# Attention with relative positions and a mixture of experts: reciprocals in another step, first keys in float32, two copies on GpSimd

## The chip, the cores and the metric

The kernel runs on one core of one Trainium2 chip. The metric is the device time of one execution in microseconds (us), less being better. Five engines work side by side: TensorE (PE) multiplies, VectorE (DVE), ScalarE (ACT) and GpSimd (POOL) compute element by element, and SyncE (SP) issues most transfers.

## The reference, cut to what matters

x is 16 x 512 x 128 in float32; there are 16 heads of 8 columns.

```python
Q, K, V = heads(xn @ Wq.T + bq), heads(xn @ Wk.T + bk), heads(xn @ Wv.T + bv)  # xn = layernorm(x)
scores = einsum('bhld,bhrd->bhlr', Q, K) / sqrt(8) + einsum('bhld,lrd->bhlr', Q, rel_k)
attn = softmax(scores)
out = einsum('bhlr,bhrd->bhld', attn, V) + einsum('bhlr,lrd->bhld', attn, rel_v)
x = x + out @ Wo.T + bo
x = x + shared_experts(layernorm(x)) + top2_of_8_experts(layernorm(x))  # exact gelu, hidden 256
```

rel_k[l, r] and rel_v[l, r] are rows of a table chosen by r - l; distances beyond the table take its last row.

## The kernel before

**Stages.** The 16 batches are worked off in 8 pairs. Each pair takes 16 steps of 32 queries, each step two rounds (s, j) with j = 0 or 1. A round makes four score tiles of 128 rows (8 heads and 4 queries in each of two batches) by 512 keys. After the last pair the experts run batch by batch. Products need float32 accuracy, so most operands are split into a high and a low f16 half, and three matmuls are added up (`projected`).

**A round.** `scores` on TensorE (lines 1545, 1527, 1534) fills banks 0 to 3. VectorE takes each tile's negated maximum (line 1030, `maxima`), ScalarE the exponential with its row sum (line 793). TensorE meanwhile multiplies the values and relative values of an older step (lines 1612 and 1622), transposes the probabilities of the round before (line 1592), and VectorE and ScalarE copy these out of PSUM (lines 1035 and 783). TensorE's last transpose of a round carries the waits for the next scores (`next_scores_wait`). GpSimd spreads the queries into the stationary tiles stat_hi, stat_lo and stat_rel of a later step (lines 557, 567, 573).

**Pieces.** Some rounds have one further piece of work in bank 1, which starts once the second exponential of the round has read that bank (`round_read`). In (0, 1) and (1, 0) it is this pair's value projection (lines 1507 to 1509), in (8, 0) and (8, 1) the transposes of the next pair's normalised rows (line 1469, then ScalarE's copy in line 716 and VectorE's subtraction in line 970), later its keys and queries. The last pair has no next one; its pieces, from (7, 0), belong to the first batch's experts, and the one in (7, 1) needs the reciprocals.

**Row sums.** Each pair's row sums lie in one of two buffers. `reciprocals` on VectorE makes their reciprocals in three dependent instructions (lines 1225, 1228, 1230): the reciprocal, the high f16 half, the low half. It runs for the pair before at the end of round (0, 1). ScalarE waits for it once, at the start of a pair, for the buffer that was done a pair ago.

**The start.** For pair 0 all is done in one piece. TensorE transposes the rows and projects queries, then keys in f16 (lines 1474 to 1476) and transposes natural queries (line 1492). ScalarE copies the keys out of PSUM (line 756) into `first_k`, and from there makes k_hi with two biases (lines 761, 762); VectorE makes q_hi's rest q_lo (line 997), splits the queries (lines 1010, 1012), and makes k_lo from `first_k` (lines 1002, 1003); GpSimd makes the low part of q_split (line 547). The sync queue brings q_hi's halves into q_twice in four transfers for the first 128 queries of each batch (line 384), then q_lo's (line 387), then keys. The first scores wait for stat_rel, which needs q_rel (lines 776, 1017) from VectorE and ScalarE. VectorE does head_scaled (line 1354) on the way.

The order is written out by hand; every engine has its own queue and works it off in order, held only by semaphores.

Of the kernel before, what the change touches and what calls it, by code (L numbers as in the profile page):

```python
# [107 lines left out]
def attention_ffn(nc, x, w_qkv, cols, rows, wo_t, bo, rk_win, rv_win, rw, rb, w1, w2, b2,  # L108
                  sw1, sw2, sb2, b1_cols, consts, rel_scratch, out):
    with ExitStack() as ctx:  # L110
# [43 lines left out]
        mv = sb("mv", [P, 8, 2])  # L154
        var_eps = sb("var_eps", [P, 8])
        rstd = sb("rstd", [P, 8])
        xn_t = sb("xn_t", [P, TOK])

        xn_split = xn_t[:].bitcast(F16).rearrange("p (a c) -> p a c", a=2)
# [31 lines left out]
        probs_t = [sb(f"probs_t{i}", [P, QUADS, RT, P]) for i in range(2)]  # L191


        first_k = attn_t[:, TOK:2 * TOK].rearrange("p (b c) -> p b c", b=2)

        w1_s = attn_t[:, 3 * TOK:3 * TOK + EXPERTS * HID].rearrange("p (e h) -> p e h", e=EXPERTS)
        w2_s = attn_t[:, 3 * TOK + EXPERTS * HID:3 * TOK + 2 * EXPERTS * HID].rearrange("p (e k d) -> p e k d", e=EXPERTS, k=2)
# [46 lines left out]
        loaded, w1_loaded, w2_loaded, ffn_loaded = sem("loaded"), sem("w1_loaded"), sem("w2_loaded"), sem("ffn_loaded")  # L244
        w_high, w_low, ffn_setup = sem("w_high"), sem("w_low"), sem("ffn_setup")
        qkv_high, qkv_low, xn_low = sem("qkv_high"), sem("qkv_low"), sem("xn_low")
        setup_dve = sem("setup_dve")
        setup_pool = sem("setup_pool")

# [67 lines left out]
        def _(sp):  # L317
# [56 lines left out]
                    cols = slice((4 * twos + a) * P, (4 * twos + a + 1) * P)  # L374
                    sp.dma_start(rel_scratch[bass.ds(row, 32), cols], rel_t[32 * a:32 * a + 32, twos % 2, :]).then_inc(rel_stored[twos % 2], 16)

            def first_queries(cols, landed):
                def part(rows):
                    return rows.rearrange("p (b c) -> p b c", b=2)[:, :, cols]

                sp.wait_ge(hi_ready, START + 2)
                for half in range(2):
                    for copy in range(2):
                        sp.dma_start(part(q_twice[64 * copy:64 * copy + 64, half, :]), part(q_hi[64 * half:64 * half + 64, :])).then_inc(landed, 16)
                sp.wait_ge(q_low_ready, START + 2)
                for half in range(2):
                    sp.dma_start(part(q_lo_pair[64 - 64 * half:128 - 64 * half, 1, :]), part(q_lo[64 * half:64 * half + 64, :])).then_inc(landed, 16)
# [93 lines left out]
                load_rel(b)  # L481


            first_queries(slice(0, P), first_q_landed)
            first_keys(sp, 1, slice(0, L), first_k_landed)
            first_queries(slice(P, L), q_copies_landed)
            for b in range(2):
                first_keys(sp, b, slice(L, KEYS), k_copies_landed)
            pair_windows(0, 0, True, True)
# [20 lines left out]
        def _(pool):  # L510
# [100 lines left out]
            def pair_steps(pair, first, ahead):  # L611

                if first:
                    pool.wait_ge(first_q_landed, COPIES * 16)
                else:
                    pool.wait_ge(q_copies_landed, START + (pair + 1) * COPIES * 16)
                for s in range(STEPS):
                    if first and s == GROUP_STEPS:
                        pool.wait_ge(q_copies_landed, START + COPIES * 16)
                    if s >= 2 or not first:  # L620

                        pool.wait_ge(score_done, START + (pair * STEPS + s - 1) * QUADS)
                    if s == STEPS - 1:

                        spread_relative(s)
                        spread_high(s)
                        spread_low(s)
                    else:
                        spread_high(s)
                        spread_low(s)  # L630
                        if s == 0:
                            pool.wait_ge(q_rel_ready, START + pair * 4 + 4)
                        spread_relative(s)
                    if s == 2:
                        for b in range(2):
                            far_values(pair, b)
                    chunk = chunk_in(pair, s, 3)
                    if chunk is not None:
                        low_weights(chunk)
                    if not ahead and s in (3, 4):  # L640
                        spread_heads(s - 3)
                    if ahead and s == 8:
                        deviations(pair + 1)
                        normalised(pair + 1)
                    if ahead and s == 14:
                        split_low(pair + 1, 0)
                    if ahead and s == 15:
                        for b in range(2):
                            low_queries(pair + 1, b)
                        split_low(pair + 1, 1)  # L650
                    if not ahead and s == 12:
                        deviations_after(0)
                    if not ahead and s == 15:
                        gate_exponentials(0)

            deviations(0)
            for i, split in enumerate((wq_split, wk_split, wv_split)):
                pool.wait_ge(qkv_high, i + 1)
                nc.gpsimd.tensor_tensor(split[:, 1, :], w_qkv_s[:, i, :], split[:, 0, :], ALU.subtract).then_inc(qkv_low, 1)
            pool.wait_ge(setup_dve, SETUP_FIRST)  # L660
            for b in range(2):
                split_low(0, b)
            pair_steps(0, True, True)
# [47 lines left out]
        def _(act):  # L711
# [38 lines left out]
                act.wait_ge(q_ready, START + b + 1)  # L750
                nc.scalar.activation(q_hi[:, b * L:(b + 1) * L], q_f[:, b * L:(b + 1) * L], ACT.Copy).then_inc(hi_ready, 1)

            def first_plain_keys(b, bank):

                act.wait_ge(proj_done, START + 2 + b + 1)
                nc.scalar.activation(first_k[:, b, :], ps[:, bank, :], ACT.Copy, scale=1.0 / W_SCALE).then_inc(k_ready, 1)

            def first_high_keys(b):

                act.wait_ge(k_ready, START + b + 1)  # L760
                nc.scalar.activation(k_hi[0][:, b, FAR_COLS:KEYS], first_k[:, b, :], ACT.Identity, bias=bks_col[:, 0:1])
                nc.scalar.activation(k_hi[0][:, b, 0:FAR_COLS], first_k[:, b, FAR * P:L], ACT.Identity, bias=bk_far_col[:, 0:1]).then_inc(hi_ready, 1)

            def high_weights(n):

# [125 lines left out]

            act.wait_ge(loaded, 16 * LOADS)

            for i, (split, scale) in enumerate(((wq_split, 1.0), (wk_split, SCALE), (wv_split, 1.0))):
                nc.scalar.activation(split[:, 0, :], w_qkv_s[:, i, :], ACT.Copy, scale=W_SCALE * scale)
                nc.scalar.activation(w_qkv_s[:, i, :], w_qkv_s[:, i, :], ACT.Copy, scale=W_SCALE * scale).then_inc(qkv_high, 1)
            for half in range(2):
                rows_t(0, half, half)
            nc.scalar.activation(rk_split[:], rk3, ACT.Copy).then_inc(rk_high, 1)

            act.wait_ge(setup_dve, SETUP_FIRST)
            for b in range(2):
                first_high_queries(b)
            for b in range(2):
                first_plain_keys(b, 2 + b)
                natural_queries(0, b, 6 + b)
                first_high_keys(b)
            first_keys(act, 0, slice(0, L), first_k_landed)
            for b in range(2):
                relative_queries(0, b, 0, 2 * b, True)  # L910
# [16 lines left out]
        def _(dve):  # L927
# [68 lines left out]
                cols = slice(b * L, (b + 1) * L)  # L996
                nc.vector.tensor_tensor(q_lo[:, cols], q_f[:, cols], q_hi[:, cols], ALU.subtract).then_inc(q_low_ready, 1)

            def first_low_keys(b):

                dve.wait_ge(hi_ready, START + 2 + b + 1)
                nc.vector.scalar_tensor_tensor(k_lo[:, b, FAR_COLS:KEYS], first_k[:, b, :], bks_col[:, 0:1], k_hi[0][:, b, FAR_COLS:KEYS], ALU.add, ALU.subtract)
                nc.vector.scalar_tensor_tensor(k_lo[:, b, 0:FAR_COLS], first_k[:, b, FAR * P:L], bk_far_col[:, 0:1], k_hi[0][:, b, 0:FAR_COLS],
                                               ALU.add, ALU.subtract).then_inc(k_low_ready, 1)

            def split_queries(pair, b):
# [66 lines left out]
            def score_round(pair, parity, s, j, first, ahead):  # L1073
# [36 lines left out]
                else:  # L1110
# [3 lines left out]
                    if piece == "rows1":  # L1114
                        low_rows_t(pair + 1, 1, PIECE_BANK)
                    evacuate(pair, s, 1)
                if (s, j) == (0, 1) and not first:
                    reciprocals(pair - 1, 1 - parity)
                if not ahead:
                    if (s, j) == (8, 1):  # L1120
# [251 lines left out]
                first_low_queries(b)  # L1372
            for b in range(2):
                split_queries(0, b)
                first_low_keys(b)
            setup()
            for b in range(2):
                first_relative_queries(b, 2 * b + 1)
# [22 lines left out]
        def _(pe):  # L1401
# [441 lines left out]
                pe.wait_ge(xn_low, START + b + 1)  # L1843
                project_queries(0, b, 4 + b)
            for b in range(2):
                project_keys(0, b, 2 + b)
                natural_queries(0, b, 6 + b)
            for half in range(2):
                relative_queries(0, 0, half, half)
# [85 lines left out]
```

## Time and profile before

| | us |
|---|---|
| median of 3 runs | 2062.05 |
| lowest and highest | 2060.28, 2062.34 |
| the profiled execution | 2061.96 |
| its span, first to last instruction | 2060.2 |
| TensorE busy | 2018.7 (98%) |
| VectorE busy | 1606.0 (78%) |
| ScalarE busy | 1509.4 (73%) |
| GpSimd busy | 1216.6 (59%) |

Busy time counts each instruction as long as it is reported. Matmuls overlap in the pipeline, so the 98% do not mean that TensorE works at its peak. The rows below come from one profiled execution; times in them count from the span's start.

### The profile page before, as it was taken

Reading aid. Unit: us, or ns where it says so; the run is one execution under the profiler, and the core shown is the slowest. Engines: PE = TensorE matmul, PEld = TensorE weight load, DVE = VectorE, ACT = ScalarE, POOL = GpSimd, SP = SyncE. Lnnn points to the kernel's source line nnn. Section 1 sums busy time; section 2 is a strip of 40 time slices with the busy share of each in tenths; the row PEclk is TensorE's granted clock in tenths of the full one; section 3 lists DMA queues with packets and bytes.
Section 4 is the critical chain, followed back from the end, with each engine's and each line's share of the span. In section 5 each row is a group of like instructions: output and inputs, shape, how many; then the busy total and the mean of one; then the engine's idle time right before and its main releaser. Section 6 shows DMA issues by size and latency. Waiting matters only on the chain.

```text
span 2060.2 us, 86849 instructions
## 1 busy us (share of the span) xinstructions
PE 2018.7 (98%) x37410; PEld 1497.1 (73%) x37410; DVE 1606.0 (78%) x3739; ACT 1509.4 (73%) x3341; POOL 1216.6 (59%) x1285
## 2 busy tenths in 40 slices
PE   4999999999999999999999999999999999999999
PEld 3777777777777777777777777777777777777776
DVE  6877897788778877887897788778877777676765
ACT  4767677777677766667667767667666888888887
POOL 4554465456445645554455446445443889988897
PEclk8999999999999999999999999999999999999999
DMA  4212311321231122112211321223122221222120
GB/s 112 74 47 69 83 46 48 83 66 49 57 82 57 47 69 73 55 46 69 77 53 46 84 67 46 57 73 68 46 54 50 27 32 27 28 27 33 24 31 12
DMA packets 256658, 113.05 MB, mean 55 GB/s; under 512 B 143018, under 2 KB 253492, under 8 KB 256276
## 3 DMA queue, kind: packets, MB, share of 16 engines
q1 hardware_dynamic: 255796, 107.10, 21.5%
q8 instruction: 296, 4.85, 1.0%
q14 instruction: 86, 0.70, 0.1%
q10 hardware_dynamic: 480, 0.39, 0.1%
HBM read 83.34 MB, written 8.39 MB: 45 GB/s over the span
## 4 chain that ended last, share of the span: by engine, by line
PE 90%; DVE 5%; ACT 2%; POOL 1%; issue 1%; DMA 0%; SPq 0%; ACTq 0%; DVEq 0%; POOLq 0%
PE ps L1592 21%; PE ps L1527 12%; PE ps L1612 10%; PE ps L1534 9%; PE ps L1622 8%; PE ps L1545 7%; PE ps L1810 3%; PE ps L1812 3%; PE ps L1811 3%; PE ps L1792 3%; PE ps L1794 3%; PE ps L1793 3%; ACT probs L793 1%; DVE keys L1270 1%; PE ps L1501 1%
## 5 line engine op out<-in xcount | busy, mean ns | idle before, releaser
L793 ACT ACTIVATE probs<-ps,neg_max 128x512 f32<-128x512 f32 x1024 | 690.5, 686 | 345.4 <-DVE neg_max L1030 345.3
L1030 DVE TENSOR_REDUCE neg_max<-ps 128x1 f32<-128x512 f32 x1024 | 635.3, 682 | 148.3 <-PE ps L1534 144.3
L557 POOL TENSOR_TENSOR stat_hi<-q_twice,mask8h 128x1024 f16<-128x1024 f16 x128 | 242.5, 1895 | 533.9 <-PE ps L1534 487.9
L1592 PE MATMUL ps<-const,probs 128*128 128x128 f32 x4096 | 500.6, 275 | 4.1 <-issue 1.6
L1592 PEld LDWEIGHTS ps<-const,probs 128*128 128x128 f32 x4096 | 450.2, 141 | 36.1 <-issue 20.3
L1035 DVE COPY probs_t<-ps 128x512 f32<-128x512 f32 x512 | 340.4, 685 | 109.1 <-PE ps L1592 103.7
L783 ACT ACTIVATE probs_t<-ps 128x512 f32<-128x512 f32 x512 | 280.0, 595 | 121.1 <-PE ps L1592 117.1
L690 POOL TENSOR_TENSOR probs_t<-probs,probs_t 128x1024 f16<-128x1024 f32 x160 | 341.4, 2157 | 30.6 <-ACT probs_t L875 29.9
L1527 PE MATMUL ps<-keys,stat_hi 128*32 128x512 f16 x4096 | 318.1, 383 | 0.0
L1534 PE MATMUL ps<-rk_split,stat_rel 96*32 96x512 f16 (+2 forms) x4096 | 281.7, 340 | 0.0
L573 POOL TENSOR_TENSOR stat_rel<-q_rel,mask4h 96x1024 f16<-96x1024 f16 x128 | 251.3, 1963 | 46.2 <-PE ps L1534 30.5
L1310 DVE SCALAR_TENSOR_TENSOR keys<-ps,comb,keys 128x128 f32<-128x128 f32 x640 | 179.4, 343 | 112.6 <-PE ps L1812 112.1
L1622 PE MATMUL ps<-probs_t,rv_step 128*32 128x128 f32 x6656 | 226.4, 273 | 0.7 <-DMA rv_step<-in_rv_win 0.7
L1612 PE MATMUL ps<-probs_t,v_s 128*32 128x128 f32 x6656 | 226.1, 272 | 0.0
L1810 PE MATMUL ps<-w_h,probs_t 128*128 128x128 f16 x1280 | 222.6, 219 | 0.7 <-POOL probs_t L690 0.7
L1812 PE MATMUL ps<-w_h,probs_t 128*128 128x128 f16 x1280 | 222.6, 219 | 0.0
L1811 PE MATMUL ps<-w_l,probs_t 128*128 128x128 f16 x1280 | 222.5, 219 | 0.0
L869 ACT ACTIVATE probs<-ps,b_s 128x512 f32<-128x512 f32 x320 | 202.2, 683 | 27.7 <-PE ps L1794 23.8
L793 ACT ACTIVATION_READ_ACCUMULATOR probs<-ps,neg_max 128x1 f32 x1024 | 207.3, 202 | 0.0
L1527 PEld LDWEIGHTS ps<-keys,stat_hi 128*32 128x32 f16 x4096 | 91.3, 96 | 158.4 <-issue 108.5
L1612 PEld LDWEIGHTS ps<-probs_t,v_s 128*32 128x32 f32 x6656 | 185.0, 109 | 22.9 <-issue 1.1
L567 POOL TENSOR_TENSOR stat_lo<-q_lo_pair,mask8h 128x128 f16<-128x128 f16 x512 | 189.8, 403 | 0.0
(192 smaller groups left out, 2861.4 us busy)
## 6 DMA issues: line engine op xcount, KB each, us to landing
rv_step<-in_rv_win SPq DMA_DIRECT2D x128, 512.0 KB, 3.8
keys<-keys SPq DMA_DIRECT2D x56, 96.0 KB, 2.9
x_pair<-in_x SPq DMA_DIRECT2D x8, 512.0 KB, 4.6
rel_scratch<-rel_t SPq DMA_DIRECT2D x256, 16.0 KB, 2.9
x_pair<-in_x SPq DMA_DIRECT2D x16, 256.0 KB, 3.2
x_pair<-rel_scratch SPq DMA_DIRECT2D x64, 64.0 KB, 4.1
out<-keys SPq DMA_DIRECT2D x16, 256.0 KB, 2.3
q_twice<-q_hi SPq DMA_DIRECT2D x28, 128.0 KB, 2.4
```

What stands on the lines that cost most here:

```text
L690: nc.gpsimd.tensor_tensor(hid_l[:, n % SLOTS, :, :], hid[:, n % SLOTS, :, :], hid_h[:, n % SLOTS, :, :], ALU.subtract).then_inc(hid_low, 1)
L793: nc.scalar.activation(probs[:, q, :], ps[:, i, :], ACT.Exp, bias=neg_max[:, q:q + 1], accum_out=row_sum[parity][:, s * QUADS + q:s * QUAD ...
L1030: nc.vector.tensor_reduce(neg_max[:, q:q + 1], ps[:, i, :], op=ALU.max, axis=AX_X, negate=True).then_inc(max_done, 1)
L1035: nc.vector.tensor_copy(probs_t[s % 2][:, q, :, :].rearrange("p r c -> p (r c)"), ps[:, tr_bank(q), :]).then_inc(evac_dve, 1)
L1527: nc.tensor.matmul(ps[at:at + 32, q % IN_ROUND, :], stat_hi[s % 2][:, half, b, q, :], group_keys(k_both[parity][:, half, b, :], group), st ...
L1534: last = nc.tensor.matmul(ps[32 * g:32 * g + 32, q % IN_ROUND, L - near:L], stat_rel[s % 2][:, q, g, :, :].rearrange("k l h -> k (l h)"), ...
L1592: last = nc.tensor.transpose(ps[:, bank, rt * P:(rt + 1) * P], probs[:, q, rt * P:(rt + 1) * P], ident)
L1612: nc.tensor.matmul(ps[32 * g:32 * g + 32, AV_BANK, b * P:(b + 1) * P], values[:, 32 * g:32 * g + 32], cols, start=rt == 0, stop=rt == RT - ...
L1622: last = nc.tensor.matmul(ps[32 * g:32 * g + 32, AV_BANK, (2 + half) * P:(3 + half) * P], rv_step[:, RT - 1 - block, q * 32:q * 32 + 32], ...
L1810: nc.tensor.matmul(y, hid_h[:, place, k, rows], w2_h[:, e, k, :], start=k == 0, stop=False)
L1811: nc.tensor.matmul(y, hid_h[:, place, k, rows], w2_l[:, e, k, :], start=False, stop=False)
L1812: last = nc.tensor.matmul(y, hid_l[:, place, k, rows], w2_h[:, e, k, :], start=False, stop=k == 1)
```

## The change

There are three edits. The reciprocals of the pair before now stand at the end of round (7, 1), and in the last pair at the end of (4, 1), instead of (0, 1). The keys of pair 0 are projected by one float32 matmul per batch, from a float32 copy of the transposed rows (`first_xn`) and of the scaled weights (`first_wk`), both made by ScalarE; k_hi and k_lo are then made straight from PSUM, and `first_k` is gone. Of the four transfers that bring the first queries' high half into q_twice, the two that stay on their own partitions become copies on GpSimd; the transfers to the other partitions and those of the low half stay.

```diff
@@ sync: first_queries(cols, landed, both)
-                    for copy in range(2):
+                    for copy in range(2) if both else (1 - half,):
                         sp.dma_start(part(q_twice[64 * copy:64 * copy + 64, half, :]), part(q_hi[64 * half:64 * half + 64, :])).then_inc(landed, 16)
-            first_queries(slice(0, P), first_q_landed)
+            first_queries(slice(0, P), first_q_landed, False)
@@ gpsimd
-                    pool.wait_ge(first_q_landed, COPIES * 16)
+                    pool.wait_ge(first_q_landed, 4 * 16)
@@ gpsimd, between the low weights and split_low(0, b)
             pool.wait_ge(setup_dve, SETUP_FIRST)
+            pool.wait_ge(hi_ready, START + 2)
+            for half in range(2):
+                rows = slice(64 * half, 64 * half + 64)
+                nc.gpsimd.tensor_copy(q_twice[rows, half, :].rearrange("p (b c) -> p b c", b=2)[:, :, 0:P],
+                                      q_hi[rows, :].rearrange("p (b c) -> p b c", b=2)[:, :, 0:P]).then_inc(first_high, 1)
+            pool.wait_ge(first_high, 2)
@@ scalar
-            def first_plain_keys(b, bank):
-                act.wait_ge(proj_done, START + 2 + b + 1)
-                nc.scalar.activation(first_k[:, b, :], ps[:, bank, :], ACT.Copy, scale=1.0 / W_SCALE).then_inc(k_ready, 1)
-            def first_high_keys(b):
-                act.wait_ge(k_ready, START + b + 1)
-                nc.scalar.activation(k_hi[0][:, b, FAR_COLS:KEYS], first_k[:, b, :], ACT.Identity, bias=bks_col[:, 0:1])
-                nc.scalar.activation(k_hi[0][:, b, 0:FAR_COLS], first_k[:, b, FAR * P:L], ACT.Identity, bias=bk_far_col[:, 0:1]).then_inc(hi_ready, 1)
+            def first_high_keys(b, bank):
+                act.wait_ge(proj_done, START + 2 + b + 1)
+                nc.scalar.activation(k_hi[0][:, b, FAR_COLS:KEYS], ps[:, bank, :], ACT.Identity, bias=bks_col[:, 0:1]).then_inc(k_ready, 1)
+                nc.scalar.activation(k_hi[0][:, b, 0:FAR_COLS], ps[:, bank, FAR * P:L], ACT.Identity, bias=bk_far_col[:, 0:1]).then_inc(hi_ready, 1)
...
+            nc.scalar.activation(first_wk[:], w_qkv_s[:, 1, :], ACT.Copy, scale=SCALE).then_inc(first_rows, 1)
...
             for half in range(2):
                 rows_t(0, half, half)
+            for half in range(2):
+                act.wait_ge(xn_low, START + half + 1)
+                nc.scalar.activation(first_xn[:, half * L:(half + 1) * L], ps[:, half, :], ACT.Copy).then_inc(first_rows, 1)
             nc.scalar.activation(rk_split[:], rk3, ACT.Copy).then_inc(rk_high, 1)
...
             for b in range(2):
-                first_plain_keys(b, 2 + b)
                 natural_queries(0, b, 6 + b)
-                first_high_keys(b)
+                first_high_keys(b, 2 + b)
@@ vector: first_low_keys(b, bank), both lines
-                ... k_lo from first_k[:, b, :], the bias and k_hi
+                ... k_lo from ps[:, bank, :], the bias and k_hi
@@ vector: score_round
-                if (s, j) == (0, 1) and not first:
+                if (s, j) == (7 if ahead else 4, 1) and not first:
                     reciprocals(pair - 1, 1 - parity)
@@ tensor: the first pair
             for b in range(2):
-                project_keys(0, b, 2 + b)
+                pe.wait_ge(first_rows, b + 2)
+                nc.tensor.matmul(ps[:, 2 + b, :], first_wk[:], first_xn[:, b * L:(b + 1) * L], start=True, stop=True).then_inc(proj_done, 1)
                 natural_queries(0, b, 6 + b)
```

## Rows read from the trace of the kernel before

**Rows 1.** The page, part 4: the chain that ended last.
```profile
PE 90%; DVE 5%; ACT 2%; POOL 1%; issue 1%; DMA 0%; SPq 0%; ACTq 0%; DVEq 0%; POOLq 0%
```

**Rows 2.** Waits of TensorE: us in total, times, longest us.
```profile
PE ps L1507 <- ACT probs L793: 6.0, 9, 1.4
```

**Rows 3.** Timeline, pair 2, second step: start us, us, instruction, idle before.
```profile
428.60 0.10 PEld L1507 LDWEIGHTS ps<-wv_split,xn_t 128*128 128x128 f16 x1 [0.20 <-issue]
...
431.28 0.94 DVE L1225 RECIPROCAL row_sum<-row_sum 128x128 f32<-128x128 f32 x1
...
431.93 0.28 PE L1534 MATMUL ps<-rk_split,stat_rel 96*32 96x256 f16 x4
...
432.22 0.73 POOL L552 TENSOR_TENSOR v_far<-v_s,rows_s 128x256 f32<-128x256 f32 x1
...
433.27 2.48 DVE L1030 TENSOR_REDUCE neg_max<-ps 128x1 f32<-128x512 f32 x4
...
435.55 0.10 PEld L1507 LDWEIGHTS ps<-wv_split,xn_t 128*128 128x128 f16 x1 [0.88 <-ACT probs L793]
```

**Rows 4.** Timeline, pair 2, eighth to ninth step.
```profile
509.38 1.48 POOL L567 TENSOR_TENSOR stat_lo<-q_lo_pair,mask8h 128x128 f16<-128x128 f16 x4
...
510.42 2.48 DVE L1030 TENSOR_REDUCE neg_max<-ps 128x1 f32<-128x512 f32 x4 [1.35 <-PE ps L1534]
...
510.81 1.97 POOL L573 TENSOR_TENSOR stat_rel<-q_rel,mask4h 96x1024 f16<-96x1024 f16 x1
...
512.91 0.42 PEld L1469 LDWEIGHTS ps<-const,x_pair 128*128 128x128 f32 x4 [0.20 <-ACT probs L793]
...
514.65 0.68 DVE L970 TENSOR_TENSOR xn_t<-ps,xn_t 128x512 f16<-128x512 f32 x1
```

**Rows 5.** Line 1228 by source: ns min/median/max.
```profile
L1228 DVE TENSOR_SCALAR inv_all<-row_sum x8: 227/771/776, 239.1 to 1582.6; 128x128 f16<-128x128 f32 x8
```

**Rows 6.** Line 567 by source.
```profile
L567 POOL TENSOR_TENSOR stat_lo<-q_lo_pair,mask8h x512: 394/401/1371, 26.1 to 1553.1; 128x128 f16<-128x128 f16 x171
```

**Rows 7.** Timeline, last pair, fifth to sixth step.
```profile
1443.24 1.96 POOL L573 TENSOR_TENSOR stat_rel<-q_rel,mask4h 96x1024 f16<-96x1024 f16 x1
...
1444.38 2.48 DVE L1030 TENSOR_REDUCE neg_max<-ps 128x1 f32<-128x512 f32 x4 [1.30 <-PE ps L1534]
...
1446.49 1.97 PE L1592 MATMUL ps<-const,probs 128*128 128x128 f32 x16
...
1447.17 0.69 ACT L793 ACTIVATE probs<-ps,neg_max 128x512 f32<-128x512 f32 x1
```

**Rows 8.** Lines 1002 and 1003 by source, then the timeline of the start.
```profile
L1002 DVE SCALAR_TENSOR_TENSOR k_lo<-attn_t,bks_col,keys x2: 742/1171/1600, 19.7 to 22.3; 128x512 f16<-128x512 f32 x2
...
L1003 DVE SCALAR_TENSOR_TENSOR k_lo<-attn_t,bk_far_col,keys x2: 472/924/1376, 21.3 to 23.0; 128x256 f16<-128x256 f32 x2
...
16.06 0.47 PE L1474 MATMUL ps<-xn_t,wk_split 128*128 128x512 f16 x1
...
16.80 0.63 PE L1492 MATMUL ps<-const,q_f 128*128 128x128 f32 x4
...
17.62 0.58 ACT L756 ACTIVATE attn_t<-ps 128x512 f32<-128x512 f32 x1
...
17.74 2.67 SPq L384 DMA_DIRECT2D q_twice<-q_hi  x4
...
19.62 1.16 POOL L547 TENSOR_TENSOR q_split<-x_pair,q_split 128x512 f16<-128x512 f32 x1 [9.15 <-DVE q_split L1012]
...
22.47 1.60 POOL L547 TENSOR_TENSOR q_split<-x_pair,q_split 128x512 f16<-128x512 f32 x1 [1.69 <-DVE q_split L1012]
...
24.03 2.07 POOL L557 TENSOR_TENSOR stat_hi<-q_twice,mask8h 128x1024 f16<-128x1024 f16 x1
...
29.99 1.95 POOL L573 TENSOR_TENSOR stat_rel<-q_rel,mask4h 96x1024 f16<-96x1024 f16 x1 [1.48 <-DVE q_rel L1017]
```

**Rows 9.** Windows: stretch, length, busy us (instructions) of each engine, clock.
```profile
23.00:43.50 20.50, 10.93 (x122) 5.36 (x123) 11.98 (x15) 6.81 (x15) 13.67 (x14) 0.50 0.40 93
```

More of the change, by code:

```diff
@@ L156, in attention_ffn @@
         rstd = sb("rstd", [P, 8])
+        first_wk = sb("first_wk", [P, D])
         xn_t = sb("xn_t", [P, TOK])
@@ L191, in attention_ffn @@
         probs_t = [sb(f"probs_t{i}", [P, QUADS, RT, P]) for i in range(2)]
-        first_k = attn_t[:, TOK:2 * TOK].rearrange("p (b c) -> p b c", b=2)
+        first_xn = attn_t[:, TOK:2 * TOK]
         w1_s = attn_t[:, 3 * TOK:3 * TOK + EXPERTS * HID].rearrange("p (e h) -> p e h", e=EXPERTS)
@@ L246, in attention_ffn @@
         qkv_high, qkv_low, xn_low = sem("qkv_high"), sem("qkv_low"), sem("xn_low")
+        first_rows, first_high = sem("first_rows"), sem("first_high")
         setup_dve = sem("setup_dve")
@@ L375, in store_rel, with first_queries @@
                     sp.dma_start(rel_scratch[bass.ds(row, 32), cols], rel_t[32 * a:32 * a + 32, twos % 2, :]).then_inc(rel_stored[twos % 2], 16)
-            def first_queries(cols, landed):
+            def first_queries(cols, landed, both):
                 def part(rows):
@@ L481, in load_next @@
                 load_rel(b)
-            first_queries(slice(0, P), first_q_landed)
+            first_queries(slice(0, P), first_q_landed, False)
             first_keys(sp, 1, slice(0, L), first_k_landed)
-            first_queries(slice(P, L), q_copies_landed)
+            first_queries(slice(P, L), q_copies_landed, True)
             for b in range(2):
@@ L997, in first_low_queries, with first_low_keys @@
                 nc.vector.tensor_tensor(q_lo[:, cols], q_f[:, cols], q_hi[:, cols], ALU.subtract).then_inc(q_low_ready, 1)
-            def first_low_keys(b):
+            def first_low_keys(b, bank):
                 dve.wait_ge(hi_ready, START + 2 + b + 1)
-                nc.vector.scalar_tensor_tensor(k_lo[:, b, FAR_COLS:KEYS], first_k[:, b, :], bks_col[:, 0:1], k_hi[0][:, b, FAR_COLS:KEYS], ALU.add, ALU.subtract)
-                nc.vector.scalar_tensor_tensor(k_lo[:, b, 0:FAR_COLS], first_k[:, b, FAR * P:L], bk_far_col[:, 0:1], k_hi[0][:, b, 0:FAR_COLS],
+                nc.vector.scalar_tensor_tensor(k_lo[:, b, FAR_COLS:KEYS], ps[:, bank, :], bks_col[:, 0:1], k_hi[0][:, b, FAR_COLS:KEYS], ALU.add, ALU.subtract)
+                nc.vector.scalar_tensor_tensor(k_lo[:, b, 0:FAR_COLS], ps[:, bank, FAR * P:L], bk_far_col[:, 0:1], k_hi[0][:, b, 0:FAR_COLS],
                                                ALU.add, ALU.subtract).then_inc(k_low_ready, 1)
@@ L1374, in _ @@
                 split_queries(0, b)
-                first_low_keys(b)
+                first_low_keys(b, 2 + b)
             setup()
```

## The prediction

> **What bounds the kernel now.** I read the page's chain of waits first. It is 90% TensorE, with VectorE at 5% and ScalarE at 2% [rows 1]. So in steady state an edit on another engine is worth only the TensorE idle time that it makes or removes. The view of who waited for whom comes next. Of the waits inside the loop one group stands out: the value projection (line 1507) waits 6.0 us in nine places for an exponential of ScalarE, at most 1.4 at once [rows 2]. The timeline then shows what makes the projection late in the second step of a pair, and what holds the start. The reader should see two separate places: a stall once in each of seven pairs, made by the reciprocals, and the start-up chain, which lasts 32 us.
>
> **Reciprocals, what leaving step 0 gives.** In pair 2 they start at 431.28 and the maxima after them at 433.27, so the three instructions hold VectorE for 1.99 us [rows 3]. The last matmuls of that half step's first tile (line 1534) began at 431.93 and are reported 0.28 long. So without the reciprocals the maxima begin at about 432.25, 1.0 us earlier. The second exponential, for whose bank the projection waits, comes as much earlier. The weight load of the projection has 0.88 us of idle time before it, against 0.20 in the half step before, where nothing is late: 0.68 us is stall [rows 3]. As 1.0 is more than 0.68, all of it goes, and TensorE's own queue is what is last again. Pairs 1 to 7 carry reciprocals in step 0, so 7 x 0.68 = 4.8 us.
>
> **What they cost in the eighth step.** They stand behind the copies of (7,1), where VectorE has 1.35 us idle before the maxima of (8,0) at 510.42 [rows 4]. They are queued ahead of these maxima, and the exponentials, the row transposes (line 1469) and the low half of the rows (line 970) all follow. They begin at 510.42 - 1.35 = 509.1, less the 0.1 by which two such instructions overlap. The reciprocal takes 0.97 us with the step to the next (0.94 is its own time [rows 3]), to 509.96. The scaling is the unsure part: it took 0.227 us at least and 0.771 in the middle of eight [rows 5]; in step 0 it ended with GpSimd's v_far, 432.22 + 0.73 [rows 3]. So it waits for a GpSimd instruction that is running. At 509.96 GpSimd is in its four stat_lo, one per 0.36 us from 509.38, and stat_rel begins at 510.81 [rows 4]. One of 512 stat_lo took 1371 ns where the middle is 401 [rows 6]: VectorE does get in between two of them. I take it so: wait to 510.10, scaling to 510.33, one more stat_lo to 510.69, low half to 510.98, maxima at about 510.9. They are D = 0.5 us late. The row transposes at 512.91 come 2.5 us behind the first maximum, two exponentials and a little slack, by my estimate 0.2 us. The low rows' subtraction at 514.65 hangs on the fourth exponential with some 0.1 to spare, and TensorE's last transpose waits for it. Cost D - 0.1 = 0.4 us, in six pairs (1 to 6): 2.4 us. Bounds: without any wait D is below 0.1 and the cost nothing; if the last of the three falls behind stat_rel, which lasts 1.97, D is 2.6 and the cost 2.5 each.
>
> **The last pair.** Behind (4,1) there is 1.30 us idle before the maxima at 1444.38 [rows 7]. The reciprocal ends at 1443.08 + 0.9 = 1443.98, and here stat_rel runs from 1443.24 for 1.96: the scaling ends at 1445.26, the low half at 1445.55, the maxima start at 1445.5, 1.1 late. The last exponential of that half step starts at 1447.17 and is reported 0.8 later, at 1447.96; 1.1 later that is 1449.07. The last of the 16 transposes, which waits for it, starts at 1446.49 + 1.97 - 0.27 = 1448.19. Cost 0.9 (0.4 if the scaling gets in before stat_rel). Steady state together: 4.8 - 2.4 - 0.9 = 1.5 us gained.
>
> On this port the Trainium skill, "SBUF — State Buffer", section "Who interferes with whom", says that a VectorE instruction in a two-port mode, or with two SBUF inputs, and a GpSimd instruction lock one port pair, and the one that issues second blocks. The trace agrees: the scaling's two durations above. The rule speaks against both GpSimd edits, and a scaling behind stat_rel is the third rival.
>
> **First pair's keys.** The chain before the first score runs through VectorE and GpSimd: stat_rel starts at 29.99 after 1.48 us of waiting for q_rel [rows 8]. VectorE's low keys took 1600 and 742 ns (512 columns), 472 and 1376 (256 columns), and the longer of each pair lie beside q_split on GpSimd. They now read PSUM in place of an SBUF copy; a subtraction with one PSUM input took 0.68 [rows 4]. I take the blocked time as gone: 0.86 + 0.90 = 1.8 us on VectorE (bounds 0 and 1.8). ScalarE loses two copies of 0.58 (line 756) behind q_hi, where it is busy, and gains one weight scaling and two row copies, which stand where it waits for GpSimd's deviations, for TensorE or for q_f. That covers them; without the cover the row copies would cost 1.2 us, twice that 0.58. TensorE does one float32 matmul of 512 columns for three in f16. Sixteen float32 transposes of 128 columns start over 1.70 us [rows 7], 0.11 each, so four times that is 0.45; the three of the first batch last from 16.06 to the next operation at 16.80, so 0.74. That is 0.3 us less per batch, and it is not last in the chain. The added wait on first_rows is for ScalarE's two row copies; TensorE has its six query matmuls to run meanwhile, so I cost it at nothing. Behind it stand the natural queries, and for them ScalarE and VectorE, so a late copy would move all of these by as much.
>
> The Trainium skill, "FP8 and Floating Point Precision", section "TensorE Precision Notes", counts four passes for true float32; by it and the f16 spacing here (0.74 / 3 = 0.25) one such matmul takes 1.0 us, the natural queries come 0.26 later instead of 0.3 earlier, and the sum would be 2060.2 in place of 2059.9. The float32 transposes in rows 7, at 0.11 us for 128 columns, do not show such a rate, though a transpose need not be a multiplication.
>
> **GpSimd's copies of the queries.** Two copies of 64 x 256 in f16. No such row exists. A stat_lo of 128 elements takes 0.40 [rows 4] and v_far of 256 elements 0.73 [rows 3]; I take 0.45, bounds 0.3 and 0.7. They start when q_hi is there, where the sync queue issues its first transfer (17.74 [rows 8]), just as VectorE subtracts q_lo and then casts q_split, and each of the two engines will hold up the other: up to 0.9 us in the chain to split_low; I take 0.5. Two of the four transfers on the sync queue go (four take 2.67 us to issue), so q_lo's two are issued 1.3 us earlier. That gives nothing by itself: stat_hi starts at 24.03, right behind the second q_split (22.47 + 1.60), with no idle time for a landing [rows 8]. What is late next is this q_split: it starts when VectorE has copied, some 0.4 earlier, and takes 1.16 unblocked, as the first one did at 19.62, instead of 1.60 [rows 8]. So stat_hi starts 0.8 to 0.9 earlier. On VectorE head_scaled, rk_split and q_rel keep their places behind it, then comes stat_rel: the first score comes 0.9 us earlier. From 23 to 43.5 the granted clock is 0.50 (1.2 GHz) [rows 9]. If it rises at the same time, what moves from behind that point to before it runs at half speed: I take 0.3 off. TensorE is busy for 10.93 us of that stretch; if the clock rises a few us earlier, some 1 to 2 us of it come back at full speed (an estimate). Setup: 0.6 us gained, bounds -0.3 and 2.0.
>
> **Sum.** 1.5 + 0.6 = 2.1 us. The profiled execution took 2061.96 us (span 2060.2, 1.76 outside it), 0.09 below the median of the runs, 2062.05. 2061.96 - 2.1 = 2059.9 us, or 0.1% less. A measurement of this kernel can tell about 0.2% (4.1 us) from no change, so this counts as no change.
>
> **Rivals.**
> 1. The reciprocals find GpSimd's port free in steps 7 and 4, or slack on the way hides D. For it: VectorE's idle 1.35 and 1.30 us nearly hold 1.5 us of work. Against: GpSimd is busy through both stretches. Then the 2.4 goes and 0.5 of the 0.9: 2059.9 - 2.9 = 2057.0. Chance 0.15.
> 2. The start gains nothing: the copies on GpSimd lock VectorE out for as long as the low keys save, or the clock takes it back. 2061.96 - 1.5 + 0.3 = 2060.8; with D's cost also at 0.65 per pair, 2062.3. Chance 0.2.
> 3. Slower: in step 7 the low half of the reciprocals lands behind stat_rel. It decides from the point where it is issued after 510.81 in the frame of [rows 4]; I put it at 510.36, 0.45 us before. Then 6 x 2.5 in place of 2.4 adds 12.6: 2072.5. For it: in the last pair just this happens to the scaling. Chance 0.05.
> 4. Moving the reciprocals back gives nothing, because the projection waits for another engine then. Against: in (0,1) the same instructions show only 0.20 us idle. 2061.96 + 2.4 + 0.9 - 0.6 = 2064.7. Chance 0.03.
>
> **How the numbers follow.** The forecast has 0.57 and reaches from 2058.3 to 2061.3. The range is 2057.0 to 2062.3: from rival 1 to the end of rival 2. Faster by over 0.2% (below 2057.9) is rival 1 and an earlier clock: 0.17. Slower by over 0.2% (above 2066.2) is rival 3: 0.05. The rest, 0.78, is within.
>
> **What would show it.** Right: line 1507 no longer waits for ScalarE in pairs 1 to 7; the maxima of (8,0) start 0.5 us later against the scores of their half step; in the last pair TensorE waits about 0.9 us in (5,0); stat_rel of the first step starts near 29.1. Wrong: the scaling takes 0.23 us in the eighth step (rival 1), or a VectorE instruction of over 1.5 us stands there (rival 3); q_rel begins no earlier than before (rival 2).

## The result, and the profile after

The changed kernel takes 2073.32 us (median of 4 runs, 2072.13 to 2074.96), the kernel before 2061.76 beside it: the ratio is 1.0057, with a 95% interval of 1.0044 to 1.0069. It is 11.6 us slower. The forecast was 2059.9 and no change; its range ended at 2062.3. The profiled execution took 2073.51 us, its span is 2071.6 (before: 2060.2). The time is near the 2072.5 of the third rival, which had a chance of 0.05 and another instruction in it than the one that waited.

The chain of waits answers to [rows 1]: TensorE still holds 90%, VectorE has 6% in place of 5%.

```profile
PE 90%; DVE 6%; ACT 2%; POOL 1%; issue 1%; DMA 0%; SPq 0%; ACTq 0%; DVEq 0%; POOLq 0%
```

TensorE's waits (us in total, times, longest us) show where it stands now. The projection's line, 1507 before, is 1516 now.

```profile
PE ps L1478 <- ACT probs L797: 14.4, 6, 2.4
...
PE ps L1516 <- ACT probs L797: 2.0, 2, 1.4
```

The 6.0 us in nine places of [rows 2] have become 2.0 in two. But in six places, one in each of pairs 1 to 6, the row transposes in (8, 0) (line 1478, before 1469) now wait 2.4 us for an exponential.

The scaling (line 1237, before 1228) by source, ns min/median/max, against the 227/771/776 of [rows 5]; the low half behind it; and stat_lo, as in [rows 6]:

```profile
L1237 DVE TENSOR_SCALAR inv_all<-row_sum x8: 226/2901/2910, 315.7 to 1594.4; 128x128 f16<-128x128 f32 x8
...
L1239 DVE SCALAR_TENSOR_TENSOR inv_all<-row_sum,inv_all x8: 292/293/293, 318.6 to 1594.7; 128x128 f16<-128x128 f32 x8
...
L570 POOL TENSOR_TENSOR stat_lo<-q_lo_pair,mask8h x512: 392/401/1377, 24.4 to 1564.8; 128x128 f16<-128x128 f16 x171
```

The timeline of pair 2 from (7, 1) to (8, 0), the place of [rows 4], shows what the 2.90 us are:

```profile
509.76 0.94 DVE L1234 RECIPROCAL row_sum<-row_sum 128x128 f32<-128x128 f32 x1
510.17 1.48 POOL L570 TENSOR_TENSOR stat_lo<-q_lo_pair,mask8h 128x128 f16<-128x128 f16 x4
510.74 2.91 DVE L1237 TENSOR_SCALAR inv_all<-row_sum 128x128 f16<-128x128 f32 x1
511.60 1.96 POOL L576 TENSOR_TENSOR stat_rel<-q_rel,mask4h 96x1024 f16<-96x1024 f16 x1
...
513.68 0.29 DVE L1239 SCALAR_TENSOR_TENSOR inv_all<-row_sum,inv_all 128x128 f16<-128x128 f32 x1
513.89 2.48 DVE L1038 TENSOR_REDUCE neg_max<-ps 128x1 f32<-128x512 f32 x4
...
516.17 0.42 PEld L1478 LDWEIGHTS ps<-const,x_pair 128*128 128x128 f32 x4 [2.68 <-ACT probs L797]
```

The scaling is issued at 510.74, in the second of four stat_lo. GpSimd goes from one instruction to the next without a pause, through two more boundaries between stat_lo's and the one before stat_rel, and the scaling ends at 513.65, 0.09 after stat_rel (511.60 + 1.96 = 513.56). So it got in at none of the boundaries. The maxima of (8, 0) start right behind it, in place of a 1.35 us idle wait for their scores, and TensorE's row transposes wait with them. All six pairs show this pattern, with scalings of 2.90 or 2.91 us.

The step that the reciprocals left, in pair 2, against [rows 3]: the maxima begin at their scores, and the weight load of the projection is back at 0.20 us idle, where it had 0.88.

```profile
433.73 2.48 DVE L1038 TENSOR_REDUCE neg_max<-ps 128x1 f32<-128x512 f32 x4 [0.90 <-PE ps L1543]
...
436.34 0.10 PEld L1516 LDWEIGHTS ps<-wv_split,xn_t 128*128 128x128 f16 x1 [0.20 <-issue]
```

The last pair, against [rows 7]. Here only stat_rel is in the way, and the scaling waits to its end:

```profile
1454.02 1.96 POOL L576 TENSOR_TENSOR stat_rel<-q_rel,mask4h 96x1024 f16<-96x1024 f16 x1
1454.76 1.30 DVE L1237 TENSOR_SCALAR inv_all<-row_sum 128x128 f16<-128x128 f32 x1
1456.10 0.29 DVE L1239 SCALAR_TENSOR_TENSOR inv_all<-row_sum,inv_all 128x128 f16<-128x128 f32 x1
1456.30 2.48 DVE L1038 TENSOR_REDUCE neg_max<-ps 128x1 f32<-128x512 f32 x4
...
1459.92 0.14 PEld L1601 LDWEIGHTS ps<-const,probs 128*128 128x128 f32 x1 [0.33 <-ACT probs L797]
```

The start, against [rows 8]:

```profile
16.10 1.02 PE L1856 MATMUL ps<-attn_t,first_wk 128*128 128x512 f32 x2
...
16.96 0.63 PE L1501 MATMUL ps<-const,q_f 128*128 128x128 f32 x4
...
17.86 1.38 POOL L667 COPY q_twice<-q_hi 64x256 f16<-64x256 f16 x2 [7.02 <-ACT q_hi L760]
...
19.31 0.73 DVE L1010 SCALAR_TENSOR_TENSOR k_lo<-ps,bks_col,keys 128x512 f16<-128x512 f32 x1
...
21.39 1.16 POOL L550 TENSOR_TENSOR q_split<-x_pair,q_split 128x512 f16<-128x512 f32 x1 [0.69 <-DVE q_split L1020]
...
22.50 1.89 POOL L560 TENSOR_TENSOR stat_hi<-q_twice,mask8h 128x1024 f16<-128x1024 f16 x1
...
28.29 1.95 POOL L576 TENSOR_TENSOR stat_rel<-q_rel,mask4h 96x1024 f16<-96x1024 f16 x1 [1.48 <-DVE q_rel L1025]
...
32.70 1.29 DVE L1038 TENSOR_REDUCE neg_max<-ps 128x1 f32<-128x512 f32 x2 [4.50 <-PE ps L1543]
```

stat_rel starts at 28.29 in place of 29.99, so the start gained 1.70 us.

**The balance**, from first maximum to first maximum of each round in the two timelines: (0, 1) and (1, 0) together lose 0.67 us in each of pairs 1 to 6 and 0.68 in the last; (7, 1) and (8, 0) together take 2.55 more in five of pairs 1 to 6 and 3.65 in pair 3; (4, 1) and (5, 0) of the last pair take 1.0 more. What pair 3 has over the others shows in its windows (length, busy us and count of PE, PEld, DVE, ACT, POOL, then the granted clock, DMA share and GB/s):

```profile
700.00:712.30 12.30, 9.90 (x219) 7.46 (x208) 10.97 (x17) 6.45 (x18) 8.62 (x11) 1.00 0.19 55
712.30:715.70 3.40, 3.40 (x33) 2.23 (x34) 3.14 (x6) 1.89 (x5) 0.00 (x0) 0.51 0.05 13
715.70:725.00 9.30, 9.07 (x195) 6.34 (x196) 6.51 (x12) 5.44 (x14) 5.25 (x6) 1.00 0.01 2
```

For 3.4 us after this one of the stalls TensorE ran at half its clock (1.2 GHz), and this (8, 0) took 1.1 us more than the others. The kernel before shows no such drop after its start. Sum: 6 x 2.55 = 15.3, less 4.7, plus 1.0, less 1.7, plus 1.1 = 11.0, of 11.4 us between the spans. The other 0.4 is not assigned. It is a net figure: from its first maximum to that of pair 1, pair 0 took 1.2 us more here, and round (11, 1) of pair 3 took 0.9 less. Both are of the size that unchanged code shows: two kernels of the next section with the pair 0 of before differ from it there by +0.7 and -0.9 us.

### The profile page after: what moved, and what is told of

Same layout as the page of the kernel before. It is cut to its first block, busy times and chain, and to the rows that moved or that the text cites. A ratio compares the mean times of both kernels' runs of the same rounds, so it can differ in the third digit from the quotient of the medians.

```text
span 2071.6 us, 86847 instructions
## 1 busy us (share of the span) xinstructions
PE 2020.8 (98%) x37408; PEld 1497.7 (72%) x37408; DVE 1619.8 (78%) x3739; ACT 1509.5 (73%) x3342; POOL 1217.4 (59%) x1287
## 4 chain that ended last, share of the span: by engine, by line
PE 90%; DVE 6%; ACT 2%; POOL 1%; issue 1%; DMA 0%; SPq 0%; ACTq 0%; DVEq 0%; POOLq 0%
PE ps L1601 22%; PE ps L1536 12%; PE ps L1621 10%; PE ps L1631 9%; PE ps L1543 8%; PE ps L1554 7%; PE ps L1819 3%; PE ps L1821 3%; PE ps L1820 3%; PE ps L1801 3%; PE ps L1802 3%; PE ps L1803 3%; DVE keys L1279 1%; DVE inv_all L1237 1%; ACT probs L797 1%; PE ps L1510 1%
```

## The experiments

Theory: the move of the reciprocals is the whole loss, because the scaling waits until GpSimd has nothing more to run. Rivals: another edit is at fault; the place in the round is, and not the meeting with GpSimd; or the form of the scaling is, with its one input in SBUF.

**Each part alone.** In the kernel before:

```diff
-                if (s, j) == (0, 1) and not first:
+                if (s, j) == (7 if ahead else 4, 1) and not first:
                     reciprocals(pair - 1, 1 - parity)
```

> The kernel before with the reciprocals alone moved, to (7,1) and in the last pair to (4,1). Theory A (the reciprocals' scaling on VectorE waits for the port until GpSimd's whole run of stat_lo and stat_rel is over, 2.9 us, in each of six pairs): those pairs cost 1.9 us each net of the 0.67 saved in step 1, the last one 0.7: 2061.8 + 11.3 + 0.7 = 2073.8 us; the scaling takes 2.9 us in six of eight. Rival B (the loss comes from the edits at the start, or from their effect on the phases of the engines): about 2060.3 us, as forecast for the steady state.

It took 2073.09 us (2071.26 to 2076.82), ratio 1.0060 [1.0046, 1.0074], with a scaling of 2.90 us in five pairs and 2.63 in one. The move alone is a loss of 11.7 us, as large as the whole. The same line put back in the kernel after leaves the start edits alone:

> The changed kernel with the reciprocals back in (0,1), so that only the float32 keys and GpSimd's two copies are left of the change. Theory A: no loss; the first maximum comes at 32.7 instead of 34.4 us, so 2061.8 - 1.7 = 2060.1 us, up to 2061.3 if the 1.2 us that pair 0 was longer belong to these edits. Rival B: most of the 11.6 us, about 2072 us.

2058.23 us (2056.84 to 2059.66), ratio 0.9986 [0.9977, 0.9995]: the start edits gain some 3 us, and no other edit is at fault. Only 1.5 of the 3.2 us stand at the first maximum (32.88 against 34.41); where the rest comes from isn't shown. Nor do the two parts add up: 11.7 - 3.2 = 8.5, where 11.6 was measured, a difference that the three intervals (2 to 3 us to each side) still allow.

**The form of the scaling.** In the kernel after:

```diff
-                nc.vector.tensor_scalar(high, row_sum[parity][:], INV_SCALE, None, ALU.mult)...
+                nc.vector.tensor_tensor(high, row_sum[parity][:], inv_scale[:].broadcast_to([P, STEPS * QUADS]), ALU.mult)...
```

> The changed kernel with the scaling written as a product of two SBUF tensors (the second one column, read 128 times) instead of one tensor and a number; the place is the same. Theory A (a form that uses both ports for one tensor needs GpSimd's queue empty, a form with two inputs gets in between two instructions): the scaling takes 0.3 to 0.7 us in pairs 1 to 6, the maxima of (8,0) are 0.5 late instead of 2.7, and the time is 2073.3 - 6 x 2.2 = about 2060 us. Rival C (VectorE has no room there whatever the form: 1.5 us of work before 1.35 us of idle time, and the exponentials, row transposes and copies behind it): at least 2068 us. Rival D (any VectorE instruction with a second port waits as long): 2073.

2074.0 us, ratio 1.0068 [1.0054, 1.0082]. The scaling, now with two inputs, waits just as long (2.93 to 2.95 in six pairs; timeline of pair 2). So it isn't the form with one input:

```profile
511.14 2.94 DVE L1239 TENSOR_TENSOR inv_all<-row_sum,inv_scale 128x128 f16<-128x128 f32 x1
511.97 1.96 POOL L578 TENSOR_TENSOR stat_rel<-q_rel,mask4h 96x1024 f16<-96x1024 f16 x1
```

**Another step, where GpSimd is nearly done.** In the kernel after:

```diff
-                if (s, j) == (7 if ahead else 4, 1) and not first:
+                if (s, j) == ((9, 1) if ahead else (0, 1)) and not first:
```

> The changed kernel with the reciprocals at the end of (9,1) in pairs 1 to 6 and at (0,1), as before, in the last pair. There stat_rel of GpSimd ended 0.4 us before the next maxima, and the next round (10,0) has no further piece. Theory A: the scaling waits 0.1 to 0.3 us, the maxima of (10,0) are 0.2 to 0.4 late, within what the exponentials have to spare: 2061.8 - 1.7 - 6 x 0.67 = 2056 us. Rival C (no room on VectorE in any later step): over 2061 us.

2054.57 us (2053.56 to 2056.81), ratio 0.9971 [0.9961, 0.9980]: faster than both. Pair 2, at (10, 0):

```profile
531.72 1.96 POOL L576 TENSOR_TENSOR stat_rel<-q_rel,mask4h 96x1024 f16<-96x1024 f16 x1
...
532.63 0.94 DVE L1234 RECIPROCAL row_sum<-row_sum 128x128 f32<-128x128 f32 x1
533.61 0.23 DVE L1237 TENSOR_SCALAR inv_all<-row_sum 128x128 f16<-128x128 f32 x1
533.87 0.29 DVE L1239 SCALAR_TENSOR_TENSOR inv_all<-row_sum,inv_all 128x128 f16<-128x128 f32 x1
534.08 2.48 DVE L1038 TENSOR_REDUCE neg_max<-ps 128x1 f32<-128x512 f32 x4
```

stat_rel ends at 533.68, as the scaling is issued. The same three instructions need 1.5 us here, and (9, 1) and (10, 0) are no longer than without them. Done in the kernel before, it gives the price of the place by itself:

> The kernel before with one edit: the reciprocals at the end of (9,1) in pairs 1 to 6, in (0,1) in the last pair. Theory A (leaving step 0 gives 0.68 us in each of six pairs, and nothing is late in (10,0) as the scaling meets no run of GpSimd instructions there): 4.1 us below before, 2057.7. Rival: the gain of the step-9 version comes from the start edits, and the place is worth nothing: 2061.8.

2056.94 us (2055.89 to 2059.95), ratio 0.9979 [0.9970, 0.9989]: 5.0 us gained, where 6 x 0.68 = 4.1 was expected. Between the kernel with the start edits alone and the one with step 9 besides, the same move is worth 2058.23 - 2054.57 = 3.7.

**A boundary that is really open.** Step 9 could be free for reasons of its own, so the next kernel leaves the reciprocals in (7, 1) and makes GpSimd wait, in that step alone, for its own second stat_lo before it issues the third:

```diff
                     last.then_inc(stat_ready, 1)
+                    if apart is not None and odd == 0:
+                        pool.wait_ge(stat_ready, apart)
...
-                        spread_low(s)
+                        spread_low(s, START + (pair * STEPS + s) * STAT_OPS + 2 if s == 9 and ahead and not first else None)
```

> The changed kernel, reciprocals in the same place, but GpSimd waits for its own second stat_lo before it issues the third, in the one step whose tiles it makes beside the reciprocals (pairs 1 to 6); nothing else differs. Theory A2 (a VectorE instruction that needs the port gets it only where GpSimd has no further instruction issued): the scaling gets in after the second stat_lo and takes 0.3 to 0.5 us instead of 2.9, the third stat_lo comes later by 0.3, and the time is 2073.3 - 6 x 2.1 = about 2061 us; the low half behind it may wait again for stat_rel, and then only 0.3 to 1 us per pair come back, 2068 to 2071. Rival C (VectorE's room and the chain behind it, not the port): over 2072 us with the scaling short. Rival E (the port is given to VectorE only after stat_rel whatever GpSimd's queue does): the scaling stays at 2.9 us, 2073.

2056.39 us (2055.41 to 2058.19), ratio 0.9976 [0.9966, 0.9987]. One wait on the engine that blocks, and the loss is gone. Pair 2:

```profile
507.14 0.94 DVE L1236 RECIPROCAL row_sum<-row_sum 128x128 f32<-128x128 f32 x1
507.55 1.65 POOL L570 TENSOR_TENSOR stat_lo<-q_lo_pair,mask8h 128x128 f16<-128x128 f16 x4
508.12 0.27 DVE L1239 TENSOR_SCALAR inv_all<-row_sum 128x128 f16<-128x128 f32 x1
508.42 0.51 DVE L1241 SCALAR_TENSOR_TENSOR inv_all<-row_sum,inv_all 128x128 f16<-128x128 f32 x1
508.86 2.47 DVE L1040 TENSOR_REDUCE neg_max<-ps 128x1 f32<-128x512 f32 x4
```

The scaling falls from 2.91 to 0.27 us at the same point of the same round; the four stat_lo take 1.65 in place of 1.48. (7, 1) and (8, 0) together cost 0.14 us a pair more than before, not 2.55. So the place isn't it either. In this trace GpSimd's third stat_lo starts at 508.39, as the scaling ends.

The low half shows something more. It was issued at 508.42, while the third stat_lo ran, and took 0.51 us in place of 0.29. GpSimd was given no wait before its fourth stat_lo:

```profile
508.74 0.45 POOL L570 TENSOR_TENSOR stat_lo<-q_lo_pair,mask8h 128x128 f16<-128x128 f16 x1
```

The low half ended at 508.93, before stat_rel began (509.15), and the fourth stat_lo took 0.45 us in place of 0.40. It is so in all six pairs. So VectorE can get in between two GpSimd instructions that follow each other at once, as the prediction had it; the scaling of the kernel after did not. Here GpSimd had just started again after its wait; whether that matters isn't shown.

**Earlier issue.** If the scaling waits for all that GpSimd has queued, it must wait longer the earlier it comes. Two kernels issue the reciprocals earlier in the same rounds (a move of the same two lines): the first ahead of both PSUM copies, the second between them:

> The changed kernel with the reciprocals ahead of both copies in (7,1) and (4,1), so that the scaling comes to the port some 1.3 us earlier, inside stat_hi. Theory A2: it still waits until stat_rel is over, 4 us and more, and the time is over 2080 us. Rival F (it depends on where it arrives; in the first pair a scaling that came inside stat_hi was let in at its end): the scaling ends with stat_hi, about 0.8 us, and the time is below 2066.

> The changed kernel with the reciprocals between the two copies of (7,1) and (4,1); the scaling arrives about where the first stat_lo begins. Theory A2: it waits until stat_rel is over, 3.4 us, and the second copy, for which TensorE waits, is late too: over 2076 us. Rival F (in the first pair a two-input instruction that arrived there got in behind the first stat_lo): the scaling takes 0.5 us, time below 2066.

2100.8 us (ratio 1.0192 [1.0173, 1.0211]) and 2079.83 us (1.0090 [1.0071, 1.0109]), two runs each. Pair 2 of the first of them:

```profile
512.73 4.22 DVE L1237 TENSOR_SCALAR inv_all<-row_sum 128x128 f16<-128x128 f32 x1
513.49 1.47 POOL L570 TENSOR_TENSOR stat_lo<-q_lo_pair,mask8h 128x128 f16<-128x128 f16 x4
514.92 1.95 POOL L576 TENSOR_TENSOR stat_rel<-q_rel,mask4h 96x1024 f16<-96x1024 f16 x1
```

and of the second:

```profile
509.56 1.47 POOL L570 TENSOR_TENSOR stat_lo<-q_lo_pair,mask8h 128x128 f16<-128x128 f16 x4
509.56 3.46 DVE L1237 TENSOR_SCALAR inv_all<-row_sum 128x128 f16<-128x128 f32 x1
510.98 1.96 POOL L576 TENSOR_TENSOR stat_rel<-q_rel,mask4h 96x1024 f16<-96x1024 f16 x1
```

Issued 0.76 us before the first stat_lo it takes 4.22, issued with it 3.46, issued 0.57 behind it 2.91; each time it ends 0.08 or 0.09 us after stat_rel. PSUM copies that then come late behind it make the round worse than the scaling alone would: (7, 1) takes 6.2 to 6.4 us more in the first.

That holds for pairs 1 to 6. In the last pair of the first kernel the scaling was issued inside the third of four stat_lo, and was not held:

```profile
1478.56 1.47 POOL L570 TENSOR_TENSOR stat_lo<-q_lo_pair,mask8h 128x128 f16<-128x128 f16 x4
1479.50 0.25 DVE L1237 TENSOR_SCALAR inv_all<-row_sum 128x128 f16<-128x128 f32 x1
1479.78 0.39 DVE L1239 SCALAR_TENSOR_TENSOR inv_all<-row_sum,inv_all 128x128 f16<-128x128 f32 x1
1479.99 2.00 POOL L576 TENSOR_TENSOR stat_rel<-q_rel,mask4h 96x1024 f16<-96x1024 f16 x1
```

It came 0.17 us before the end of that stat_lo; in the kernel after it came 0.19 us before the end of the second, and waited 2.9 us. So the theory is too strong as a law: what is shown is that the scaling waited for the whole run in these six pairs, and that this is the loss. Why the same instruction is let in at one boundary and not at another is not shown.

**The start, divided.** The kernel after with the reciprocals in (0, 1), and without GpSimd's copies (the four transfers of before are back):

```diff
-                    for copy in range(2) if both else (1 - half,):
+                    for copy in range(2):
...
-            for half in range(2):
-                rows = slice(64 * half, 64 * half + 64)
-                nc.gpsimd.tensor_copy(q_twice[rows, half, :]...
```

> The float32 keys alone: four transfers for the first queries as before, no copies on GpSimd, reciprocals in (0,1). It splits the 1.7 us by which the first maximum comes earlier. Theory G (the keys bring it all, by the low keys that no longer wait beside q_split; the copies only keep stat_hi from waiting for its data): the first maximum at 33.0 to 33.5 us, since stat_hi now waits for the last q_lo transfer, which lands near 23.5; 2061.4 - 1.2 = 2060.2 us. Rival H (the copies bring it): the first maximum at 34.0 or later, 2061.3 us.

2059.21 us (2056.73 to 2060.73), ratio 0.9989 [0.9979, 0.9998]; its first maximum stands at 32.43, with the copies at 32.88 (in the seven traces with copies it lies between 32.09 and 32.88). The float32 keys bring the gain, and the copies nothing that these runs can tell. The reason lies on GpSimd, whose stat_hi now waits 0.37 us for a landing and then is itself blocked while VectorE works (2.94 us in place of 1.89), while VectorE's head_scaled takes 0.18 us in place of the 1.75 that it takes beside stat_hi with the copies, and stat_rel starts at 28.02 in place of 28.46:

```profile
23.68 2.94 POOL L560 TENSOR_TENSOR stat_hi<-q_twice,mask8h 128x1024 f16<-128x1024 f16 x1 [0.37 <-DMA q_lo_pair<-q_lo_pair]
```

**The version that all of this points to**: step 9, float32 keys, no copies on GpSimd.

> The kernel after with the reciprocals at the end of (9,1) in pairs 1 to 6 and of (0,1) in the last pair, and without GpSimd's copies of the first queries (four transfers and then two, as before); the float32 keys stay. Theory A (the keys bring the whole start gain, the copies nothing): as the same kernel with the copies, which took 2054.57: 2053.5 to 2056, first maximum near 32.4. Theory B (the copies bring part of it): 1 us or more later than that.

2054.05 us (2053.38 to 2059.41), ratio 0.9965 [0.9953, 0.9977]: as fast as with the copies (2054.57), with less code. It beats the kernel before beside it by 7.9 us, the one with the copies by 6.8, and both beat the kernel after by 19.

## Why the prediction was wrong, step by step

- **Leaving step 0 (4.8 us): right.** 0.68 us was read per pair, 0.67 came in six pairs and 0.68 in the last.
- **The eighth step (2.4 us lost): wrong, and here is the error.** The step that failed is "VectorE does get in between two of them" and with it D = 0.5 us. D was 2.68 (round (7, 1) took 8.46 us instead of 5.78, first maximum to first maximum), and the cost 2.55 a pair. The prediction had this as its outer bound, "D is 2.6 and the cost 2.5 each", but tied it, there and in rival 3, to the low half landing behind stat_rel, if it is issued after 510.81. (Its paragraph on the port calls the third rival "a scaling behind stat_rel", which is what came; rival 3 was not priced by that.) The size was right and the condition wrong: it was the scaling that waited, although it was issued where it had been placed, inside the four stat_lo, and the low half behind it was free. Of the signs, the one of rival 3 came, a VectorE instruction of over 1.5 us. The difference is 6 x (2.55 - 0.4) = 12.9 us, of a miss of 13.4 between 2059.9 and 2073.3.
- **The evidence for it was one row in 512.** The maximum of 1371 ns in [rows 6] stands in the start-up; the middle of 401 says only that nobody had met the stat_lo's in the steady part. The kernel before had closer rows: an addition of VectorE with two SBUF inputs (line 1270) takes 0.69 to 2.71 us, against pairs of additions of GpSimd. They speak for both sides, where the start-up row speaks only for getting in:

```profile
1624.41 4.24 POOL L690 TENSOR_TENSOR probs_t<-probs,probs_t 128x1024 f16<-128x1024 f32 x2
...
1626.48 2.71 DVE L1270 TENSOR_TENSOR keys<-q_f,bo_row 128x512 f32<-128x512 f32 x1
...
1656.30 1.01 DVE L1270 TENSOR_TENSOR keys<-q_f,bo_row 128x512 f32<-128x512 f32 x1
```

The first was issued just before GpSimd's second addition began (1624.41 + 4.24 / 2 = 1626.53) and waited for that one too; the second got in. It is not chance here: all seven that were issued 0.04 to 0.07 us before the first addition ended took 2.68 to 2.71 us, and all six that were issued 0.46 or 0.47 us before it took 1.01 or 1.02. But timing alone doesn't explain the stat_lo's, where a scaling issued 0.19, 0.55 and 0.91 us before three boundaries in a row got in at none. With both in hand, rival 3 would have deserved about as much as the forecast.
- **The last pair (0.9 lost): right**, 1.0 measured: stat_rel alone was in the way and its end could be read.
- **First keys and queries (0.6 gained): right in kind, too small.** The low keys took 731 to 747 and 469 to 476 ns: all of the 1.8 us taken as blocked time went. The first maximum came 1.7 us earlier, not 0.9; with the reciprocals in their old place the gain was 3.2 us on the median. GpSimd's copies took 0.84 and 0.49 us, not 0.45 each, but lie where GpSimd was idle before (9.15 us ahead of the first q_split, [rows 8]), and VectorE's first cast and copy beside them took 0.62 and 0.38 us in place of 0.43 and 0.29. So 0.5 for them in the chain was too much. The term for the clock did not show: the half-speed stretch ended at 39.9 us in place of 43.5, but from the first maximum to the end of step 2 pair 0 gained 0.04 us.
- **The float32 matmul** starts at 16.10 and the next operation at 16.96: 0.86 us, not 0.45. That is four times the 0.21 between f16 matmuls in the kernel before, so the trace agrees with the four passes of the Trainium skill, "FP8 and Floating Point Precision", section "TensorE Precision Notes"; float32 transposes are no measure for it. It cost nothing, since VectorE and GpSimd end this chain.
- **A price that no part had:** the half-speed stretch behind one stall, 1.1 us.
- **The forecast of "no change"** failed with the eighth step alone: 2073.3 - 12.9 = 2060.4, which is within the stated range.

## What to carry to other kernels

When an instruction that shares a port is moved, lay it against the whole unbroken run of the other engine's instructions and price it as if it ended with that run; count on a gap only where the other engine is seen to wait. Boundaries without such a wait were open in some places and closed in others, and no rule that these traces show tells which. A duration that is rare in the trace (one of 512) says that a case can occur, not that it will. The cheapest cure may be on the blocking side: one wait of GpSimd for its own last instruction left 0.14 us of the 2.55 lost in each pair.

## What the runs showed of the hardware

The Trainium skill, "SBUF — State Buffer", section "Who interferes with whom", has the engine that issues first hold the shared pair for its whole instruction, and the other fully blocked. A wait of one instruction agrees with it (the scaling beside v_far, 0.77 us). The runs show more: the scaling on VectorE stayed blocked over up to five boundaries between GpSimd instructions (stat_hi, four stat_lo, stat_rel; 4.22 us), in each of pairs 1 to 6 of five kernels, and got in where GpSimd waited on a semaphore (0.27 us) or had ended (0.23). It also got in without such a wait: the low half before the fourth stat_lo, six times of six, where GpSimd waits before its third; the scaling in the last pair of the kernel with the reciprocals ahead of both copies; the addition at 1656.30; and the case in the start-up. What decides stays open; so does whether any semaphore wait would do, or only one that lets the engine run empty.

Behind the long stalls the granted clock fell to half for a few us: in one of six pairs of the kernel after, in three of the kernel with the move alone and of that with the other form, in four with a scaling of 3.46 us, and in all six with one of 4.22. It did not fall after the start in the seven kernels without such a stall. These counts are from one profiled execution of each kernel. So part of the price of a stall comes behind it: in some of the places where the stall is short, and in all six where it was longest.
